# Source one-hots of a neighbour count built by five equal compares in place of two unequal ones

## What is computed

```python
N_NODES, N_EDGES = 3125, 100000
deg = segment_sum(ones_like(dst), dst, num_segments=N_NODES)
d_invsqrt = clip(deg, 1.0, None)[:, None] ** -0.5
h = THETA[0] * feat
for k in range(1, len(THETA)):
    scaled = feat * d_invsqrt
    agg = segment_sum(scaled[src], dst, num_segments=N_NODES)
    feat = feat - agg * d_invsqrt
    h = h + THETA[k] * feat
```

## Time and profile before

| | us |
|---|---|
| median of three executions | 6337.69 |
| lowest and highest of them | 6327.33, 6339.27 |
| the profiled execution | 6332.13 |
| span of its trace | 6330.3 |
| VectorE busy in the span | 3231.4 |
| GpSimd busy | 3245.7 |
| TensorE busy | 4164.1 |
| the scatter, first start to last start | 379.6 to 1426.2 |
| the count's visits, first to last compare | 419.3 to 926.7 |

### The profile page before, as it was taken

How to read it: one execution, slowest core, us unless ns; L and a number is a source line. 1 busy time by engine, 2 the same in 40 slices (tenths; PEclk the granted TensorE clock), 3 DMA queues, 4 the chain that set the end, 5 groups by cost and what they waited for, 6 DMA issues and landing times. The chain is left out here.

```text
span 6330.3 us, 89423 instructions
## 1 busy us (share of the span) xinstructions
PE 4164.1 (66%) x19143; PEld 2784.5 (44%) x19144; DVE 3231.4 (51%) x7314; ACT 792.8 (13%) x2439; POOL 3245.7 (51%) x3323
## 2 busy tenths in 40 slices
PE   6969880006899778888846668888898744444431
PEld 5844430002699544444435534544444433333331
DVE  6967760008897465666567741222122255554556
ACT  1210010001200022222210010010010012222210
POOL 0047777770000277777722017636647457777761
PEclk7569995558899888888869979989899855555555
DMA  4311120002566577777745546766677543333331
GB/s 122 101 59 33 43 53 2 2 2 93 196 242 247 151 210 216 213 213 215 215 138 147 153 174 237 245 223 233 206 266 244 171 138 81 82 82 81 82 84 53
DMA packets 516122, 909.59 MB, mean 144 GB/s; under 512 B 100755, under 2 KB 349832, under 8 KB 476628
## 3 DMA queue, kind: packets, MB, share of 16 engines
q1 hardware_dynamic: 410094, 741.27, 35.9%
q0 software_dynamic: 105824, 165.90, 11.6%
HBM read 680.21 MB, written 226.65 MB: 143 GB/s over the span
## 5 line engine op out<-in xcount | busy, mean ns | idle before, releaser
L2771 POOL DMA_INDIRECT l_gathered<-l_table,l_st x816 | 775.7, 951 | 869.5 <-issue 785.0
L1793 POOL DMA_INDIRECT l_edges_by_src<-l_by_src,l_edges_st x816 | 786.4, 964 | 728.1 <-SPq L1887 479.7
L440 POOL DMA_INDIRECT by_src<-src_rec,src_pos x784 | 808.8, 1032 | 560.3 <-ACT attr_turned L742 321.6
L1793 POOL DMA_INDIRECT l_edges_by_src<-l_q,l_edges_st x816 | 777.2, 952 | 347.4 <-issue 242.9
L2840 PE MATMUL psum<-l_blocks,l_rows 128*128 128x512 f32 (+1 forms) x2016 | 819.3, 567 | 2.3 <-ACT l_rows L2782 2.3
L1872 PE MATMUL psum<-l_rows,l_edges_hot_t 128*128 x1632 | 443.2, 453 | 564.9 <-DVE l_scores L2910 541.9
L1691 PE MATMUL psum<-pair_hot_weight,pair_hot_dst 128*128 128x512 f32 x1200 | 641.9, 677 | 173.5 <-DVE pair_hot_dst L1681 166.0
L2799 DVE TENSOR_SCALAR l_hot<-iota,l_loc,l_weight 128x128 f32<-128x128 f32 x816 | 223.3, 357 | 928.0 <-PE psum L2856 924.7
L1872 PEld LDWEIGHTS psum<-l_rows,l_edges_hot_t 128*128 128x128 f32 x1632 | 379.2, 330 | 633.1 <-issue 633.1
L2840 PEld LDWEIGHTS psum<-l_blocks,l_rows 128*128 128x128 f32 x2016 | 375.8, 200 | 419.6 <-issue 414.8
L2507 PE MATMUL psum<-l_scaled,l_counts 128*128 128x128 f32 x3750 | 424.3, 277 | 18.8 <-ACT l_scaled L2432 18.8
(11 more groups left out here) (484 smaller groups left out, 5584.9 us busy)
## 6 DMA issues: line engine op xcount, KB each, us to landing
l_blocks<-pair_blocks SPq DMA_DIRECT2D x216, 1024.0 KB, 5.5
l_counts<-counts SPq DMA_DIRECT2D x65, 1600.0 KB, 6.9
pair_blocks<-pair_block SPq DMA_DIRECT2D x75, 1024.0 KB
l_edges_loc<-loc_by_tile SPq DMA_DIRECT2D x416, 128.0 KB, 3.0
l_rows<-l_edges_by_src SPq DMA_DIRECT2D x204, 256.0 KB
l_sum_rows<-l_rows SPq DMA_DIRECT2D x204, 256.0 KB, 2.6
attr_then_counts<-in_edge_attr SPq DMA_DIRECT2D x14, 1568.0 KB
counts<-attr_then_counts SPq DMA_DIRECT2D x13, 1600.0 KB
```

The costliest lines, as they stand in the source:

```text
L440: pool.indirect_dma_start(table, bass.IndirectOffsetOnAxis(ap=pos[:, e:e + 1], axis=0), rec[:, e, :], None).then_inc(s_out[g % R], 16)
L1793: pool.indirect_dma_start(a[:, r, g, :], None, table_src, bass.IndirectOffsetOnAxis(ap=st[:, r, g:g + 1], axis=0))\
L2771: pool.indirect_dma_start(sent[:, p, g, :], None, by_type, bass.IndirectOffsetOnAxis(ap=st[:, p, g:g + 1], axis=0))\
```

## The change

`one_hots` makes the 3200 columns of `hot_src` in five compares of 640 columns, each with one value per partition and no second operation. `hot_dst` stays as it was. Six compares a visit now raise `s_hot` where three did, and TensorE's wait is counted accordingly. Nothing else changes, neither on GpSimd nor on TensorE.

```diff
-    WEIGHED = 19 * P
+    SHARE = NP // 5
@@
             v.wait_ge(s_used, n + 1)
             v.nop(nofuse=True)
-            for cols, one in ((slice(0, WEIGHED), k.ones[:, 0:1]), (slice(WEIGHED, NP), None)):
+            for col in range(0, NP, SHARE):
+                cols = slice(col, col + SHARE)
                 v.tensor_scalar(hot_src[:, bass.ds(place, 1), cols].rearrange("p a c -> p (a c)"), iota[:, cols],
-                                shifted[:, 0, bass.ds(t, 1)], one, ALU.is_equal,
-                                *((ALU.mult,) if one is not None else ())).then_inc(s_hot, 1)
+                                shifted[:, 0, bass.ds(t, 1)], None, ALU.is_equal).then_inc(s_hot, 1)
@@
-                    pe.wait_ge(s_hot, (t + b) * 3 + 3)
+                    pe.wait_ge(s_hot, (t + b) * 6 + 6)
```

## The result

The changed kernel takes **6490.54 us** (median of four runs, 6482.93 to 6495.89), the kernel before in the same comparison 6336.08. The ratio is 1.0248, with a 95% interval of 1.0232 to 1.0264. The forecast was 6297, its range ended at 6325, and the time lies 166 us above that. The profiled execution took 6482.93 us, with a span of 6481.1.

What follows compares the result with a forecast made beforehand. GpSimd's scatter sends were taken to bound the block, the count having slack. Of 57.7 us excess, 331 sends at 0.05 us would lose 16.5, leaving 41 us gained: 6337.7 - 41 = 6297 us, range 6287 to 6325.

Steps and rivals of the forecast that it cites:

- The scatter ends the block: End of the stage: GpSimd's last send, not the count, ends the block, so only the sends' pace matters.
- 57.7 us: Sends beside the count: 363 sends, each 0.159 us over those behind it; all the change could give back.
- The count had slack: Count of compares and matmuls: over at about 935 us, 492 us of slack before the scatter's end.
- The new wait of a send: Sends beside 640-column compares: 0.05 us extra each, bounded by 0.02 and 0.147; 16.5 us lost in all.
- GpSimd gets in between two compares that follow each other without a gap: VectorE's back-to-back compares: a waiting send gets in between them, read from two places in the earlier trace.
- the upper bound from half a pace: Wait of a send until the running compare's end: half the 0.295 us pace, 0.147 us; 45 us lost, 6325 us.
- The row taken as nearest: Later layer's sends beside 512- and 128-column compares: 964 ns mean over 944 free, 0.020 us extra at 63% cover.
- Rival 2: Sends beside the count: GpSimd gets in once a visit, 95 us lost, 37 us slower, 6375 us; chance 0.07.
- sends of 1.35 us in step with the visits: Sign of rival 2 in the count: each send lasts 1.35 us and keeps step with one visit.
- The other half of rival 2: Compares with two values per partition: the second value, costing 65 ns, may be what opens the gap.
- The terms of the visit: Count's visit: 5 x 0.295 + 0.16 = 1.63 us free of waits, plus 0.14 held up by GpSimd, 1.77 us.
- rival 1: Sends in step with compares: each waits most of a fresh compare, 0.22 us; 6 us slower, 6344; chance 0.08.

Runs made afterwards that it cites:

- g1: The changed kernel with the second value (column of ones) given back to all five 640-column compares: 6301.24 us, kernel before 6330.31; under the slower condition ratios 1.0087 to 1.0096.
- g2: The kernel before without the second value on its wide compare (2432 and 768 columns, both one-value): 6332.67 us, kernel before 6330.31.
- g3: The changed kernel with the second value on only the first of its five compares: 6382.04 us, kernel before 6330.31.
- h: Changed kernel with five unequal one-value compares, two of 1600, or six with 128 columns mid-row: 7480.37, 7471.50, 7505.60 us; kernel before 7479.20.
- i: Changed kernel with five unequal one-value compares, or six with 128 columns mid-row, and g1's kernel again: 7487.15, 7513.68, 7545.09 us; kernel before 7480.33.
- k: g1's kernel again, and the changed kernel with five unequal one-value compares or six with 128 columns mid-row: 7583.21, 7522.42, 7538.36 us; kernel before 7517.95.
- e4: The changed kernel with a multiplication by the constant 1.0 on all five compares, no second value read: 7514.43 us, ratio to the kernel before 1.0002, slower condition.
- g5: The changed kernel with one one-value compare of 3200 columns in place of five: 6404.78 us, kernel before 6330.31.
- e1: The changed kernel with the second value on all five compares, under the slower condition: 7570.94 us, ratio to the kernel before 1.0084.

## Why the prediction was wrong

**Right.** The scatter ends the block before and after; 57.7 us was all that could be gained, and g1 gained 35 of it. The compare of 640 columns has 381 ns for the 378 worked out, and the sends behind the count keep 957. TensorE's granted clock during the count stayed at 0.93. The count had slack: the last compare ends at 936 instead of 927 us. GpSimd's excess moves the next block by the same amount.

**The step that failed is "The new wait of a send"**, with its sentence ahead, "GpSimd gets in between two compares that follow each other without a gap". That was drawn from two boundaries in which one side had a second value or was long, and put on one of which there was no row: two short one-value compares in a row. I took 0.05 us, with 0.147 as the upper bound from half a pace, and that bound assumed what was to be shown, that a wait ends with the running compare. The first access of the send at 427.28 misses three ends of compares, and in the 92 sends of 2.98 us the two accesses wait 2.02 us together, where such an end comes every 0.295. Measured are 215 us on the 162 sends that touch visits, 1.33 us each. The row taken as nearest, the later layer's, has compares of 559 ns with pauses between them, and was near only to g1.

**Rival 2 was the mechanism, at half its price.** It named the missing row, the second value and the one opening a visit, and had a chance of 0.07. It priced one send to a visit, 95 us lost. But my own reading of the earlier trace rows had given a send two accesses, and if only one place a visit is open, each takes one: a send of two visits. Without the good visits at each window's start, 245 x 1.643 = 403 us hold 123 sends in place of 319; with them 162, which lose 215. Of the sign that it named, "sends of 1.35 us in step with the visits", the step was there, at two visits and 2.98 us. The other half of rival 2, that the second value may be what opens the gap, fits the changed kernel against g1. It does not hold for the kernel before's widths (g2), nor in the seven good windows of g3, where sends of 0.96 us get in between one-value compares of 640 columns.

**The terms of the visit.** I took 1.77 us, 0.14 of it for VectorE's waits on GpSimd. Measured is 1.643, the 1.63 that I had worked out for a visit free of waits: VectorE waits 0.3 us for TensorE in the whole count, and beside the sends of 2.98 us GpSimd never holds it up (five compares take 1.56 us each time). That it is also TensorE's pace of 1.65 is chance. The wait that I had shared between the two engines fell on GpSimd alone. The same term for g1 would have been 5 x 0.36 + 0.16 = 1.96, where 1.98 was measured.

**How long VectorE keeps GpSimd out.** Both the forecast's upper bound and rival 1 had the wait end with a compare that is running, 0.147 us in the mean in the one and 0.22 in the other. In the changed kernel VectorE kept the send at 427.28 out across three ends of its instructions, for 1.2 us, so there the wait goes beyond the instruction, into those that follow. In g1 and g2 it is no longer than one instruction: beside the visits g1's longest send is 1.09 us, 0.13 over the free 0.96, with compares of 0.447, and g2's longest is 1.58, 0.62 over, with wide compares of 0.94 in the mean. The source row did grow by being cut in five, from 1.16 (0.83 + 0.33) to 1.48 us of starts (5 x 0.295), and the scatter hid it. It was not this that decided the time.

**Open.** What makes a boundary between short one-value compares go to VectorE. The widths alone don't (g1 has the same), nor the missing second value alone (g2), and the same boundaries are open at the start of each window and in half of g3's. Whether it is the short time between two such compares, their equal shape or their even beat, and what part the moment has at which the send comes, was what h, i and k were for, and they don't tell. Untested too is the constant of e4 under the first condition, which would tell the second operation from the second value, and whether g1's gain holds when timed several times there.

## What to carry to other kernels

When GpSimd's indirect DMAs run beside chains of short VectorE compares, read at which ends of compares a send got in and how many such openings it needs, and look for a row of exactly the pair of instructions that the change will put in sequence. If there is none, the pace of the compares, 0.295 us here, does not bound the wait: the two accesses of a send waited 2.02 us together. The distance to the next boundary that is known to be open, times the accesses of a send, would have covered it, 2 x 1.64 us. An operation that looks superfluous, here a multiplication by one, can go with what leaves the other engine room (1000 ns a send with it in g1, 1541 without it in the changed kernel), and engines that fall into step can stay in the bad step to the end of a loop (92 sends of 2.98 us, in every one of the 13 windows).

## What the runs showed of the hardware that I had not expected

In stretches of three kernels a send locks to exactly two visits (2.98 us in the changed kernel, 3.10 in g3, 2.42 in g5), and the same code falls into the good or the bad step from window to window (g3). An identical program, the kernel before, took 6330.31 us in one comparison and 7480.33 in another on the same chip. Under the slower condition the loops of VectorE and TensorE hardly advance beside GpSimd's sends: 44 of the 245 visits are done when the sends end, in each of the fourteen runs there (e1 to e4 and h to k; of the kernel before there is only the time). The changed kernel itself was not run under it, but e4, with compares of the same length, takes the kernel before's time (1.0002).
